# Four triangle layers on one core: the last stages' variance from two bf16 parts of the squares instead of f32 squares

## The reference

```python
xn = layernorm(groupnorm(x))                      # layer 3 has no layernorm here
left, right = (xn @ Wl) * sigmoid(xn @ Wlg), (xn @ Wr) * sigmoid(xn @ Wrg)
gate = sigmoid(xn @ Wg)
t = einsum('bikd,bjkd->bijd', left, right)        # layers 2 and 3: over the first index
t = layernorm(t) * w + b                          # over the 64 channels
x = x + (t * gate) @ Wo                           # layers 1 and 3: gate * (t @ Wo + b)
```

## Time and profile before

| | |
|---|---|
| median of 3 runs | 1652.48 us (1646.8 to 1660.31) |
| the profiled execution | 1650.46 us |
| its span, first to last instruction | 1648.7 us |
| mean granted TensorE clock | 0.953 of full |
| busy, PE / PEld / DVE / ACT / POOL | 83% / 52% / 58% / 65% / 23% of the span |
| PE, variance of the last stages (L595) | 1152 records, 141.6 us busy |
| weight loads for them | 1152 records, 161.2 us busy |
| normalisations of the last stages (L1034, DVE) | 192, 107.1 us busy |

### The profile page before, as it was taken

The page is one execution under the profiler, slowest core; times in us unless marked ns, Lnnn a source line. Parts: engine busy times, 40 slices in busy tenths (PEclk is TensorE's granted clock), DMA queues, the critical chain, the costliest instruction groups (busy, mean ns, idle before and its releaser), DMA issues. The chain is left out here.

```text
span 1648.7 us, 43788 instructions
## 1 busy us (share of the span) xinstructions
PE 1376.3 (83%) x12950; PEld 863.2 (52%) x12950; DVE 960.9 (58%) x2784; ACT 1070.1 (65%) x2381; POOL 384.3 (23%) x345
## 2 busy tenths in 40 slices
PE   0899998898788888989905888889889677798998
PEld 0444444576344446767603555567566333475665
DVE  6477774288588882247703666621467788710555
ACT  0688884498688882269805888832677688722654
POOL 0233330154233330024402333300233100000334
PEclk9999998899799999999956999999999899998999
DMA  7011114387223223568784333234899544245899
GB/s 255 25 48 48 48 48 128 109 247 240 87 96 95 95 77 119 148 191 258 229 196 111 96 95 95 77 117 144 225 290 298 183 142 142 98 145 163 262 296 282
DMA packets 206502, 249.31 MB, mean 151 GB/s; under 512 B 29025, under 2 KB 196321, under 8 KB 206433
## 3 DMA queue, kind: packets, MB, share of 16 engines
q1 hardware_dynamic: 206432, 248.42, 50.6%
HBM read 139.83 MB, written 108.53 MB: 151 GB/s over the span
## 5 line engine op out<-in xcount | busy, mean ns | idle before, releaser
L968 DVE SCALAR_TENSOR_TENSOR lr<-ps,mask,act_out 128x128 f32 (+5 forms) x1152 | 282.7, 311 | 81.5 <-ACT act_out L713 78.4
L1120 POOL TENSOR_TENSOR rstd<-ve,half_col 128x6 f32<-128x6 f32 x144 | 190.1, 1321 | 463.9 <-DVE ve L941 463.9
L490 PE MATMUL ps<-w_parts,val 64*128 64x256 bf16 (+1 forms) x2112 | 213.8, 303 | 38.8 <-DVE lr L968 34.2
L713 ACT ACTIVATE act_out<-ps 128x384 f32<-128x384 f32 x384 | 190.1, 496 | 20.0 <-PE ps L497 17.6
L1151 POOL TENSOR_TENSOR new_ring<-val,res_ring 128x384 f32<-128x384 f32 x96 | 95.7, 998 | 460.0 <-DVE val L1055 399.7
L490 PEld LDWEIGHTS ps<-w_parts,val 64*128 64x128 bf16 (+1 forms) x2112 | 90.4, 111 | 189.9 <-DVE lr L968 152.1
L595 PEld LDWEIGHTS ps<-k,sq 128*128 128x128 f32 x1152 | 161.2, 195 | 50.4 <-issue 2.1
L761 ACT ACTIVATE in_ring<-ps 128x768 f32<-128x768 f32 (+1 forms) x64 | 51.9, 810 | 183.7 <-PE ps L546 162.6
L1034 DVE TENSOR_TENSOR xn<-ps,cen 128x384 f32<-128x384 f32 x192 | 107.1, 558 | 104.3 <-PE ps L603 103.5
L1140 POOL TENSOR_TENSOR val<-act_out,gate_ring 128x384 f32<-128x384 f32 x96 | 95.9, 999 | 278.9 <-ACT act_out L795 210.1
L588 PE MATMUL ps<-in_ring,k 128*128 128x384 f32 x288 | 130.8, 540 | 31.9 <-DMA in_ring<-t_scratch 31.6
(11 more groups left out here) (97 smaller groups left out, 2451.8 us busy)
## 6 DMA issues: line engine op xcount, KB each, us to landing
gate_scratch<-gate_ring SPq DMA_DIRECT2D x192, 192.0 KB, 2.3
gate_ring<-gate_scratch SPq DMA_DIRECT2D x96, 384.0 KB, 4.0
in_ring<-x_scratch SPq DMA_DIRECT2D x144, 192.0 KB, 2.4
in_ring<-t_scratch SPq DMA_DIRECT2D x144, 192.0 KB, 4.8
res_ring<-x_scratch SPq DMA_DIRECT2D x72, 384.0 KB, 5.3
x_scratch<-new_ring SPq DMA_DIRECT2D x48, 384.0 KB, 3.4
t_scratch<-in_ring SPq DMA_DIRECT2D x48, 384.0 KB, 2.7
lr<-x SPq DMA_DIRECT2D x6, 1536.0 KB, 15.9
```

The costliest lines, as they stand in the source:

```text
L490: nc.tensor.matmul(banks[h][:, :, 0:P], moving(x, s)[half(h), N * r:N * r + P], proj_weights(w, h)[:, 0:2 * P], start=start, stop=stop, sk ...
L713: nc.scalar.activation(act_out[:, r, :].rearrange("p (h c) -> p h c", h=2), ps[:, 4 + 2 * r:6 + 2 * r, COLS:2 * COLS], ACT.Sigmoid).then_i ...
L968: ins = nc.vector.scalar_tensor_tensor(out5[:, h, lo // 2:hi // 2, :, m], ps[:, 4 + 2 * r + h, lo:hi].rearrange("p (a e) -> p a e", e=2), ...
L1120: nc.gpsimd.tensor_tensor(rstd[:, s % 2, :], ve[:, s % 2, :], half_col[:, :], ALU.pow)\
```

## The change

The variance of the last stages no longer takes the f32 squares as weights. `sq_high` is a view of `sq` as bf16 with every second element, that is, the upper halves of the f32 numbers, where they lie. `sq_low` is a slot of `sq_parts`, which the first stages have used; a new DVE instruction fills it with the squares minus their upper halves. PE then runs two bf16 matmuls for each chunk, one for each part, into the same sums. PE waits for a new semaphore, b2_sq_lo, which counts the subtractions, where it waited for b2_sq. In DVE's step n the new instruction is for tile n+4 and comes last.

```diff
+        sq_high = sq[:, :, :].bitcast(BF16).rearrange("p s (f e) -> p s f e", e=2)[:, :, :, 1]
+        sq_low = sq_parts[:, :, 1, :]
...
                 def variance(n, s):
-                    pe.wait_ge(b2_sq, base + n + 1)
+                    pe.wait_ge(b2_sq_lo, base + n + 1)
                     slot_free(pe, b2_std, base + n - 1)
                     for j in range(CHUNKS):
-                        mm = nc.tensor.matmul(ps[:, 6 + s % 2, 2 * j:2 * j + 2],
-                                              sq[:, s % 2, P * j:P * j + P], k_sel, start=True, stop=True)
+                        for part in (sq_high, sq_low):
+                            mm = nc.tensor.matmul(ps[:, 6 + s % 2, 2 * j:2 * j + 2],
+                                                  part[:, s % 2, P * j:P * j + P], sel_bf[:, :],
+                                                  start=part is sq_high, stop=part is sq_low)
                     mm.then_inc(b2_var, 1)
...
+                def square_low(n, s):
+                    dve.wait_ge(b2_sq, base + n + 1)
+                    nc.vector.tensor_tensor(sq_low[:, s % 2, :], sq[:, s % 2, :], sq_high[:, s % 2, :],
+                                            ALU.subtract).then_inc(b2_sq_lo, 1)
+
                 def step(n, i, s, ahead):
...
                     if ahead >= lead:
                         finish(n + lead, i + (s + lead) // RING, (s + lead) % RING)
-
+                    if ahead >= 4:
+                        square_low(n + 4, s)
+
+                square_low(0, 0)
+                square_low(1, 1)
                 inverse(0, 0)
+                square_low(2, 2)
                 inverse(1, 1)
                 normalise(0, 0)
                 normalise(1, 1)
                 inverse(2, 2)
+                square_low(3, 3)
                 if lead:
                     finish(0, 0, 0)
```

More of the change, by code:

```diff
@@ L160, in build_triangle_layers @@
             sem("b2_" + s) for s in ("z", "cen", "sq", "var", "std", "rstd", "rb", "bc", "zn"))
+        b2_sq_lo = sem("b2_sq_lo")
         b2_aff, b2_val, b2_out, b2_gated, b2_new, b2_turned = (
```

## The result

The changed kernel takes 1928.29 us (median of four runs, 1917.62 to 1937.22), the kernel before 1655.43 us in the same comparison: a ratio of 1.165, 95% interval 1.157 to 1.174. The forecast was 1870, the range 1816 to 1955. The profiled execution took 1932.4 us, its span is 1930.6.

What follows compares the result with a forecast made beforehand. The prediction took PE to bound the last stages; to the profiled 1650.5 us it added 84, 54.8, 46.4 and 34.8 for layers 0, 1, 2 and 3, making 1870.5, say 1870, range 1816 to 1955.

Steps and rivals of the forecast that it cites:

- What is moved: Last stages: PE's next variance waits for the subtraction behind finish, so PE and VectorE take turns; 3.51 us in layer 1.
- What is removed: PE's variance in the last stages: six bf16 matmuls replace three f32 ones, 0.16 us against 0.59, 0.43 less a step.
- the rival of slow loads: PE's weight loads with a stride are slow: 0.2 us on each of 176 turns, 1905 us; chance 0.03.
- The turns: One step of each last stage at full clock: 2.94, 3.51, 3.64 and 3.30 us for layers 0 to 3.
- What is added: VectorE in the last stages: one subtraction of 128x384 a tile, 0.55 us, upper end 0.56.
- the first rival: PE's clock holds at full in all four last stages: 47.6 us more in layer 0, 1834 us; chance 0.27.
- The clock: PE in the last stages: layer 0 falls to half clock, 174.6 us; the others hold at full; chance 0.45.
- a sign of being wrong: Last stages: forecast wrong if the clock differs from layer 0 mostly 0.50, others 1.00; time then moves to a rival's sum.
- The sum: Whole kernel: 1650.5 us plus 84, 54.8, 46.4 and 34.8 for layers 0 to 3 makes 1870.5.
- one f32 layer at half clock: Rival, layers 1 to 3: one falls to half clock, some 1934 to 1943 us; chance 0.20 for one or more.
- Faster: Rival, VectorE in the last stages: the subtraction gets ahead of finish, so PE doesn't wait; 1637 us, chance 0.03.

Runs made afterwards that it cites:

- the early subtraction: The changed kernel with the subtraction for tile n+4 moved from the end to the start of VectorE's step n: 1645.36 us, ratio 0.995.
- the wait alone: The changed kernel with the variance back in f32, PE still waiting for the subtraction, whose result nobody reads: 2206.36 us, ratio 1.333.
- one operand from PSUM: The changed kernel with the subtraction's first operand read from PSUM, so VectorE reads only one from SBUF (second part not true): 1876.34 us, ratio 1.136.
- the clock held as well: The changed kernel with the operation's first operand from PSUM and one more f32 matmul behind out in each step: 1826.40 us, ratio 1.106.

## Why the prediction came out as it did

**What is moved: right.** PE and VectorE take turns; the early subtraction takes that away and 283 us with it, and the wait alone brings it back.

**What is removed: right.** A block starts at 883.12 and centre at 883.33, 0.21 us for 0.59; I had put 0.16 to 0.17. The weight loads with a stride take 0.10 us, as in the earlier trace rows; the rival of slow loads falls.

**The turns: right** wherever the clock and the subtraction were as assumed. Layers 1 and 3 came out to 0.1 us, and that is luck in part: 3.51 held 0.03 us for register work that no row gave, and 3.30 was picked between 3.20 and 3.38. With one operand from PSUM layer 0 took 169.9 us for 174.6: its opening took 16.3 for 20.6, for it ran at the full clock, where I had put two of its four steps at half (by its terms such a step comes to 6.5 rather than my 6.4), and so did about four turns more; the last 36, at half clock, took 3.92 each for 3.85. With the clock held as well, 136.0, 154.3, 162.7 and 144.9 stand against 138.2, 154.4, 160.2 and 145.2, and 1826 to 1828 against the first rival's 1834.

**What is added: the term that failed.** I took 0.55 us for the subtraction from the earlier trace rows and the f32 normalisation, and set the upper end at 0.56. In layers 0 and 2 it takes 0.95 and 0.97, because GpSimd's multiply has begun first. The rows behind my bound could not show it: the normalisation reads one operand from PSUM, is a mean of the first stages, where none of the 144 subtractions overlaps an operation of GpSimd, and I did not look at what GpSimd does at that moment. The Trainium skill (SBUF — State Buffer, "🔬 SBUF: two separate sides") states it: VectorE with two SBUF inputs and a GpSimd operation that reads SBUF take a shared pair of ports in turn, each for its whole instruction, whoever starts first. The runs agree: whichever began first kept its own time, 0.55 or 0.99 us; a subtraction that began second ended 0.42 us behind the multiply, and a multiply that began second 0.86 us behind the subtraction, most of what each takes alone; with one operand from PSUM they took 548 and 995 ns.

**The clock: right for layers 0, 1 and 3, wrong for layer 2.** Layer 0 fell and stayed; layer 2 was to hold and alternated. Without the sharing it was granted 0.87, with it 0.68. I had named it as a sign of being wrong that the clock parts the layers differently, and it did. My ground for parting them, 1.7 us of long matmuls in a turn against 1.1, is not borne out: layer 2 has the same 1.7 as layers 1 and 3, and these fell too with the f32 variance, which adds work to PE. So that layers 1 and 3 held was forecast without a ground that the runs support. What parts layer 2 from them was not tried by itself. My reading of the trace before was wrong as well. A wait of 0.77 us was not the longest before a fall: some 10 us ahead of the fall at 713.8, a centre waited 3.51 us for its tile, and the matmuls behind it ran at half clock.

```profile
706.95 1.65 PE L588 MATMUL ps<-in_ring,k 128*128 128x384 f32 x2 [3.51 <-DMA in_ring<-t_scratch]
...
707.00:710.00 3.00, 3.00 (x5) 1.79 (x6) 0.00 (x0) 0.00 (x0) 0.00 (x0) 0.50 0.68 158
```

So the trace had a fall behind a long gap and another behind a short one. The rule of long gaps in the Trainium skill (TensorE: Matmul & The Clock Gate, "Why this matters for your kernels"), by which the clock would have held everywhere, is not borne out by the changed kernel: layer 0 ran at 1.00 from 318.0 to 332.5 us and fell there, with no wait ahead of it longer than 1.69 us, and then stood at half clock for 171 us with waits up to 1.83.

```profile
330.47 0.18 PE L600 MATMUL ps<-sel_bf,sq 128*128 128x2 bf16 x1 [1.69 <-DVE sq_parts L1072]
```

**The sum.** 1870.5 was forecast against the profiled execution's 1932.4: 17.4 more in layer 0, 52.8 in layer 2, 0.1 in layer 1, and 8 less outside the stretches. In layer 0 the last 36 turns, at 4.32 us for 3.85, are 17.0 of the 17.4; 0.40 us of each is the sharing. In layer 2 the sharing, with the clock that it lowers, is 38.4; the rest of the clock 12.0 (174.65 to 162.70); a turn of 3.70 rather than 3.64 the last 2.5, all as single profiles give it. The range held because it took in one f32 layer at half clock, 1934 to 1943 us, and layer 2 came near to that for two reasons of which only the clock had been thought of. That is luck, for the sharing was not foreseen.

**Faster** was ruled out because the subtraction stands behind finish, and that was so. Had it stood first, the gain would have been half of one per cent, not the 1637 us that I gave this rival: the sharing, in layer 0 above all, takes what layer 1 gains (1633 us without it).

## What to carry to other kernels

Before giving an idle engine a helper's work, write down what stands ahead of the new instruction in that engine's order, and whether any of it waits for the engine that will now wait: that alone was worth 283 us here, and moving one call undid it. Cost an added VectorE instruction by its operands, not by its size alone: with two operands in SBUF, look at what GpSimd runs at that moment and which of the two starts first. If PE must idle in every step, price the step at both clock levels: at half clock out took 1.48 us for 0.81.

## What the runs showed of the hardware

- A matmul of no use made the kernel 100 us faster, and 279 us in the f32 form of the wait, by holding the granted clock at 0.99 to 1.00 in stretches where it had been 0.53 to 0.71. With the clock the sharing between VectorE and GpSimd nearly went too.
- Layer 1 held the clock at 1.00 with turns of 3.51 us and a bf16 variance, and was granted 0.66 when the variance was f32, although PE then had more work in each turn and waits of 1.17 and 1.45 us, no longer than before; why is open.
- A lower PE clock lengthened a VectorE instruction, from 607 ns on average at 1.00 to 946 at 0.54 in layer 0: not by itself, but because it changed which of VectorE and GpSimd came first. With one operand from PSUM the instruction took 548 ns at a clock of 0.57.
